# One-hot factors of an adjacency build split as quarter and place, and strip sums made by adding transfers

## The reference, cut to what matters

```python
summed = segment_sum(h[src], dst, num_segments=n)
count = segment_sum(ones(50000), dst, num_segments=n)[:, None]
out = (summed / maximum(count, 1.0)) @ W_agg.T + h @ W_lin.T
x = x + out / maximum(norm(out, axis=-1, keepdims=True), 1e-12)
```

## Time and profile before

| | |
|---|---|
| median of 3 runs | 3345.48 us (3345.35 to 3350.49) |
| span of the profiled execution, first to last instruction | 3347.6 us |
| build, first to last matmul (L538 on 128x400) | 360.40 to 848.27 us |
| granted TensorE clock, mean over the span | 0.824 |

### The profile page before, as it was taken

One profiled execution on the slowest core, in us unless ns is written; L12 is line 12 of the kernel. 1 busy time (PEld: TensorE's weight loads), 2 busy tenths in 40 slices (PEclk: granted clock), 3 DMA queues, 4 the chain that ended last, 5 costly groups with the idle time before them and its releaser, 6 DMA issues.

```text
span 3347.6 us, 46752 instructions
## 1 busy us (share of the span) xinstructions
PE 2186.4 (65%) x12603; PEld 1297.7 (39%) x12659; DVE 2262.1 (68%) x3125; ACT 846.9 (25%) x1397; POOL 1645.1 (49%) x1455
## 2 busy tenths in 40 slices
PE   0488877777895989995963444444567665528563
PEld 0233455454453455553443111111366621107563
DVE  8999898898558720055133454444987799979777
ACT  0099433232002020022100111111244322206442
POOL 7400133333047777777104777777876777710000
PEclk9799999999997999997986555565559999965897
DMA  2000010110443523400724433345348733530453
GB/s 71 0 0 0 25 49 39 44 44 39 148 137 84 164 60 96 94 1 1 158 59 94 117 113 112 112 116 104 93 153 268 240 110 110 107 37 0 134 175 94
DMA packets 195115, 301.52 MB, mean 90 GB/s; under 512 B 120540, under 2 KB 133818, under 8 KB 194922
## 3 DMA queue, kind: packets, MB, share of 16 engines
q1 hardware_dynamic: 138986, 175.88, 16.5%
q0 software_dynamic: 40512, 62.87, 10.3%
q10 hardware_dynamic: 15552, 61.94, 6.0%
HBM read 191.65 MB, written 88.01 MB: 84 GB/s over the span
## 4 chain that ended last, share of the span: by engine, by line
PE 35%; POOL 19%; issue 16%; DVE 16%; DMA 6%; ACT 5%; ACTq 1%; DVEq 0%; SPq 0%; POOLq 0%; PEldq 0%
POOL arena L1313 18%; PE PS L538 11%; PE PS L699 9%; PE PS L884 6%; DMA arena<-T_att,idx 5%; ACT arena L514 4%; DVE arena L559 4%; PE PS L981 3%; PE PS L476 2%; DVE arena L1204 1%; PE PS L968 1%; DVE arena L374 1%; DVE arena L490 1%; POOL W L1322 1%; DVE arena L567 1%
## 5 line engine op out<-in xcount | busy, mean ns | idle before, releaser
L1313 POOL DMA_INDIRECT arena<-T_att,idx x864 | 843.7, 976 | 316.9 <-issue 224.8
L538 PE MATMUL PS<-arena 128*128 128x400 f16 (+2 forms) x4320 | 782.5, 332 | 270.0 <-issue 109.7
L538 PEld LDWEIGHTS PS<-arena 128*128 128x128 f16 (+2 forms) x4320 | 529.9, 158 | 512.9 <-issue 349.8
L1148 DVE TENSOR_REDUCE arena<-PS 128x1024 f32 (+1 forms) x432 | 502.2, 1212 | 321.6 <-PE PS L1115 321.6
L1486 POOL DMA_INDIRECT order<-arena x400 | 504.8, 1262 | 246.5 <-issue 246.5
L559 DVE TENSOR_SCALAR arena<-arena 128x1600 f16<-128x1600 f16 x448 | 385.7, 905 | 64.4 <-PE PS L538 60.4
L1115 PE MATMUL PS<-arena,pick 128*128 128x512 bf16 x812 | 315.8, 488 | 157.0 <-DVE arena L1148 143.2
L699 PE MATMUL PS<-arena 128*128 128x512 f16 (+1 forms) x1575 | 317.6, 361 | 88.3 <-issue 75.2
L633 POOL TENSOR_TENSOR rdeg<-rdeg,arena 128x1600 f32<-128x1600 f32 x48 | 159.9, 3331 | 313.4 <-ACT arena L617 313.4
L1104 PE MATMUL PS<-ident_b,score_buf 128*32 128x128 bf16 x864 | 90.0, 268 | 307.1 <-ACT score_buf L1077 297.4
L699 PEld LDWEIGHTS PS<-arena 128*128 128x128 bf16 x1575 | 147.8, 99 | 254.1 <-issue 102.3
(11 more groups left out here) (257 smaller groups left out, 2786.0 us busy)
## 6 DMA issues: line engine op xcount, KB each, us to landing
spill<-arena SPq DMA_DIRECT2D x108, 560.0 KB, 2.8
arena<-spill ACTq DMA_DIRECT2D x108, 560.0 KB, 3.9
arena<-A SPq DMA_DIRECT2D x50, 800.0 KB, 4.5
A<-arena SPq DMA_DIRECT2D x50, 400.0 KB, 2.4
arena<-A SPq DMA_DIRECT2D x50, 400.0 KB, 3.2
arena<-T_att,idx POOLq DMA_INDIRECT x864
order<-arena POOLq DMA_INDIRECT x400
T_att<-h SPq DMA_DIRECT2D x2, 1600.0 KB, 12.3
```

The lines of the kernel that those rows point to most:

```text
L538: return t.matmul(where, lhsT, rhs, start=False, stop=True, skip_group_check=True)
L1148: v.tensor_reduce(cmax[d][:, u:u + 2, bass.ds(i * SLOTS + half * GROUP + q // 2 * QUAD, QUAD)], PS[:, u * BANK:(u + 2) * BANK].rearrange(" ...
L1313: p.indirect_dma_start(out=ring1[:, b, j, :], out_offset=None, in_=T_att[d][:, :], in_offset=bass.IndirectOffsetOnAxis(ap=idx[:, d, k:k + ...
```

## The change

For each edge the band's 1,600 places are split as quarter and place in the quarter: `hi_i` = 0 to 3, `dst_low` = `dst_in` - 400 * quarter. The quarter moves into the other factor: `src_quarter` = source place + 128 * quarter. The factors of a chunk are now a 512-wide one-hot of `src_quarter` and a 400-wide one-hot of `dst_low`, both by `tensor_scalar`, in rings of 8. The four matmuls of a chunk take four different weights (128 contiguous columns each) and the same 400 columns. The sources' own instruction for 8 chunks and its semaphore are gone. `dst_sum` is cleared by a memset on POOL, and each `stage` buffer is added to it by a DMA that POOL issues and that adds as it writes (`accum_op`, fp16 read, fp32 sum); an add waits for the add of two cells before, which has the same destination. ACT reuses a `stage` buffer when both its store and its add have landed; what waited for `cell_counted` waits for all adds.

```diff
-        RING_D, RING_S, RING_A = 4, 2, 4
+        RING_D, RING_A = GROUP, 4
+        QW = BW // BQ
...
             def chunk(i, s, first):
                 if not first:
                     v.wait_ge(chunk_done, RING_D * i + s - RING_D + 1)
-                v.tensor_scalar(oh_d[s], steps_h, dst_in[:, bass.ds(RING_D * i + s, 1)], None, ALU.is_equal) \
-                    .then_inc(dst_ready, 1)
-            def sources(i, s, first):
-                if not first:
-                    v.wait_ge(chunk_done, (RING_S * i + s - RING_S + 1) * GROUP)
-                c = bass.ds((RING_S * i + s) * GROUP, GROUP)
-                v.tensor_tensor(oh_s[s], iota_8, key_h[:, c].unsqueeze(1).to_broadcast([P, P, GROUP]), ALU.is_equal) \
-                    .then_inc(src_ready, 1)
+                c = bass.ds(RING_D * i + s, 1)
+                v.tensor_scalar(oh_s[s], steps_h[:, 0:BQ * P], src_quarter[:, c], None, ALU.is_equal)
+                v.tensor_scalar(oh_d[s], steps_h[:, 0:QW], dst_low[:, c], None, ALU.is_equal).then_inc(dst_ready, 1)
             v.wait_ge(sorted_ready, 1)
-            v.tensor_copy(iota_8, steps_h[:, 0:P].unsqueeze(2).to_broadcast([P, P, GROUP]))
-            dve_link(v.tensor_copy(key_h, key[:, 1, :]))
+            dve_link(v.tensor_scalar(hi_i, dst_in, float(QW), None, ALU.is_ge))
+            for q in range(2, BQ):
+                dve_link(v.scalar_tensor_tensor(hi_i, dst_in, float(q * QW), hi_i, ALU.is_ge, ALU.add))
+            v.scalar_tensor_tensor(src_quarter, hi_i, float(P), key[:, 1, :], ALU.mult, ALU.add)
+            dve_link(v.scalar_tensor_tensor(dst_low, hi_i, -float(QW), dst_in, ALU.mult, ALU.add))
...
-            with t.Fori(0, GR[1] // RING_S) as i:
-                for s in range(RING_S):
-                    g = RING_S * i + s
...
+            with t.Fori(0, CH[1] // RING_D) as g:
+                turn = load_row(t, cell_turn[:, bass.ds(g * RING_D, RING_D)], 1, BQ * BANK * (BANDS - 1) + CELLS)
+                for j in range(RING_D):
+                    t.wait_ge(slot_free, turn[j] & 63)
+                    t.wait_ge(dst_ready, g * RING_D + j + 1)
+                    for b in range(BQ):
+                        last = add_to(t, PS[:, bass.ds((turn[j] & (BQ * BANK)) + b * BANK, QW)],
+                                      oh_s[j][:, b * P:(b + 1) * P], oh_d[j])
+                    last.then_inc(chunk_done, 1)
...
                     a.wait_ge(a_written[c % RING_A], 16 * (c // RING_A))
-                    a.wait_ge(cell_counted, c - RING_A + 1)
+                    a.wait_ge(cell_added[c % RING_A], 16 * (c // RING_A))
...
             p.wait_ge(lo_ready, 1)
+            pool_link(p.memset(dst_sum, 0.0))
             for c in range(CELLS):
                 at = dst_sum[:, c % BANDS * BW:(c % BANDS + 1) * BW]
                 p.wait_ge(cell_out, c + 1)
-                if c < BANDS:
-                    p.tensor_copy(at, stage[c % RING_A]).then_inc(cell_counted, 1)
-                else:
-                    p.wait_ge(cell_counted, c - BANDS + 1)
-                    p.tensor_tensor(at, at, stage[c % RING_A], ALU.add).then_inc(cell_counted, 1)
+                if c >= BANDS:
+                    before = c - BANDS
+                    p.wait_ge(cell_added[before % RING_A], 16 * (before // RING_A + 1))
+                p.dma_start(out=at, in_=stage[c % RING_A], accum_op=ALU.add).then_inc(cell_added[c % RING_A], 16)
```

More of the change, by code:

```diff
@@ L199, in gnn_kernel @@
         dst_in = view(6656, CH[1])
-        RING_D, RING_S, RING_A = 4, 2, 4
-        oh_d = [view(7200 + s * BW // 2, BW // 2).bitcast(F16) for s in range(RING_D)]
-        oh_s = [view(10400 + s * GROUP * P // 2, GROUP * P // 2).bitcast(F16).rearrange("p (c j) -> p c j", j=GROUP)
-                for s in range(RING_S)]
+        RING_D, RING_A = GROUP, 4
+        QW = BW // BQ
+        src_quarter, dst_low, hi_i = view(0, CH[1]), view(CH[1], CH[1]), view(2 * CH[1], CH[1])
+        oh_d = [view(7200 + s * QW // 2, QW // 2).bitcast(F16) for s in range(RING_D)]
+        oh_s = [view(8800 + s * BQ * P // 2, BQ * P // 2).bitcast(F16) for s in range(RING_D)]
         stage = [view(11424 + s * BW // 2, BW // 2).bitcast(F16) for s in range(RING_A)]
-        iota_8 = view(14624, GROUP * P // 2).bitcast(F16).rearrange("p (c j) -> p c j", j=GROUP)
-        key_h = view(14624 + GROUP * P // 2, CHUNKS // 2).bitcast(F16)
         blk = view(20800, 8 * BLK).rearrange("p (x o c n) -> p x o c n", x=2, o=2, c=2)
@@ L282, in gnn_kernel @@
         apart_ready, apart_seen = sem("apart_ready"), sem("apart_seen")
-        src_ready, dst_ready, chunk_done = sem("src_ready"), sem("dst_ready"), sem("chunk_done")
+        dst_ready, chunk_done = sem("dst_ready"), sem("chunk_done")
         cell_out, slot_free = sem("cell_out"), sem("slot_free")
-        cell_counted, dst_summed, dst_read = sem("cell_counted"), sem("dst_summed"), sem("dst_read")
+        dst_summed, dst_read = sem("dst_summed"), sem("dst_read")
+        cell_added = [sem(f"cell_added{s}") for s in range(RING_A)]
         a_written = [sem(f"a_written{s}") for s in range(RING_A)]
@@ L558, in chunk @@
                     v.wait_ge(chunk_done, RING_D * i + s - RING_D + 1)
-                v.tensor_scalar(oh_d[s], steps_h, dst_in[:, bass.ds(RING_D * i + s, 1)], None, ALU.is_equal) \
-                    .then_inc(dst_ready, 1)
-            def sources(i, s, first):
-                if not first:
-                    v.wait_ge(chunk_done, (RING_S * i + s - RING_S + 1) * GROUP)
-                c = bass.ds((RING_S * i + s) * GROUP, GROUP)
-                v.tensor_tensor(oh_s[s], iota_8, key_h[:, c].unsqueeze(1).to_broadcast([P, P, GROUP]), ALU.is_equal) \
-                    .then_inc(src_ready, 1)
-            v.wait_ge(sorted_ready, 1)
-            v.tensor_copy(iota_8, steps_h[:, 0:P].unsqueeze(2).to_broadcast([P, P, GROUP]))
-            dve_link(v.tensor_copy(key_h, key[:, 1, :]))
-            per = GROUP // RING_D
-            for s in range(RING_S):
[L575 to L584, removed]
+                c = bass.ds(RING_D * i + s, 1)
+                v.tensor_scalar(oh_s[s], steps_h[:, 0:BQ * P], src_quarter[:, c], None, ALU.is_equal)
+                v.tensor_scalar(oh_d[s], steps_h[:, 0:QW], dst_low[:, c], None, ALU.is_equal).then_inc(dst_ready, 1)
+            v.wait_ge(sorted_ready, 1)
+            dve_link(v.tensor_scalar(hi_i, dst_in, float(QW), None, ALU.is_ge))
[3 more added lines that the diff above has]
+            dve_link(v.scalar_tensor_tensor(dst_low, hi_i, -float(QW), dst_in, ALU.mult, ALU.add))
+            for s in range(RING_D):
+                chunk(0, s, True)
+            with v.Fori(1, CH[1] // RING_D) as i:
+                for s in range(RING_D):
+                    chunk(i, s, False)
         def build_pe(t):
@@ L628, in count_pool, with all_added @@
                 p.wait_ge(cell_out, c + 1)
-                if c < BANDS:
-                    p.tensor_copy(at, stage[c % RING_A]).then_inc(cell_counted, 1)
-                else:
-                    p.wait_ge(cell_counted, c - BANDS + 1)
-                    p.tensor_tensor(at, at, stage[c % RING_A], ALU.add).then_inc(cell_counted, 1)
+                if c >= BANDS:
+                    before = c - BANDS
+                    p.wait_ge(cell_added[before % RING_A], 16 * (before // RING_A + 1))
+                p.dma_start(out=at, in_=stage[c % RING_A], accum_op=ALU.add).then_inc(cell_added[c % RING_A], 16)
+        def all_added(eng):
+            for s in range(RING_A):
+                eng.wait_ge(cell_added[s], 16 * len(range(s, CELLS, RING_A)))
         DEG_PIECES = HT_BLOCKS
@@ L642, in dst_degree_pe @@
             if m == 0:
-                t.wait_ge(cell_counted, CELLS)
+                all_added(t)
             else:
@@ L1523, in _ @@
             v.wait_ge(pads_written, 16)
-            v.wait_ge(cell_counted, CELLS)
+            all_added(v)
             place_dve(v, 0)
@@ L1741, in _ @@
             a.wait_ge(h_ready, 1)
-            a.wait_ge(cell_counted, CELLS)
+            all_added(a)
             ht_act(a, 0)
```

## The result

The changed kernel takes 3324.34 us (median of 4 runs, 3321.62 to 3325.36) against 3347.31 us (4 runs, 3345.35 to 3350.49): a ratio of 0.993 [0.9916, 0.9944], **0.7% faster**. The forecast was 3293 us, 52.5 us less; 23 us came. The sign is right. The time lies above the forecast's own range (3272 to 3312) and inside the wide one (3268 to 3345) only because that one takes in the second rival. The profiled execution, which the trace shows, went from a span of 3347.6 to 3323.5 us, 24.1 us less.

A forecast was written before the change was run, and what follows sets the result against it. PE's own instruction stream sets a floor of 423 us in the 487.9 us build, DVE's stalls in POOL's adds add most of the rest; -52.5 - 6 + 2.5 + 1 + 2.5 = -52.5 us gave 3293 us, range 3272 to 3312, wide 3268 to 3345.

The forecast's parts named there:

- the second rival: Build: adds take 8.6 to 10 us, PE waits behind ACT, which waits for buffers; around 3320 us, chance 0.08.
- The adds as transfers: Strip adds in the build, moved to DMA: 6.4 us each, hidden behind PE, so 0 us of cost.
- rivals 1 to 3: Build: adds from 10.0 us bound it, 3405 us (0.14); the second rival (0.08); POOL can't issue, 4.6 ms (0.02).
- The strip adds leave POOL: Build: DVE is no longer stopped by POOL and PE runs at its own pace, 435.4 against 487.9 us: -52.5 us.
- the comparisons: DVE in the build: 0.51 us a chunk against 0.65, faster than PE's 0.8 anyway, so no gain by itself.
- PE's pace, -52.5 us: Build: 55 group steps of 7.80 us and a last 6.44 us make 435.4 us, against 487.9.
- The weights, -6 us: PE's weight loads in the build, now contiguous: 98 in place of 146 ns; -6 us, bounds -21 and 0.
- rival 4: Build: contiguous weights let PE's chunks go at their columns' pace, 54 us gained in place of 6; 3245 us, chance 0.04.
- The memset, +2.5 us: Sort stage: POOL's memset of 128 x 3200 stops DVE's comparisons; +2.5 us, bounds 0 and 2.9.
- The five instructions ahead of the build, +1.0 us: Before the build: five 448-column instructions, some 3.0 us, where 1.7 us were; +1.0 us, bounds 0 and 2.
- The end, +2.5 us: Behind the build: last store and first strip loads share DMA engines with the last adds; +2.5 us, bounds 0 and 5.

## Why the prediction was wrong in size

**The step that failed** is "The adds as transfers ... So **0 us** as long as an add takes less than about 8.6 us of the DMA engines." I asked only who waits for an add to end (ACT for a buffer, PE, DVE and ACT behind the last one), and there the answer was right: an add lands in 5.3 us (taken: 6.4), its issue takes 0.86 us (taken: 1), ACT waited for none of them (all 313.6 us of its wait are for PE, in the row of L599 above), and rivals 1 to 3 did not come. I did not ask who reads SBUF while an add runs. PE does, once a group, on its own path: +20.4 us of the build (454.4 against 434.1 with POOL's adds). The prediction had named that load as 0.9 to 1.3 us of PE's pace and taken it as fixed.

That 3324 us lies near the 3320 of the second rival, and so inside the wide range, is luck: the condition of that rival was adds of 8.6 us and more, with ACT waiting for buffers.

One reading beside this step is wrong too. By the earlier trace rows POOL's queue does not have the shorter rows: 62.87 MB in 40,512 packets are 1.55 KB each, 175.88 MB in 138,986 are 1.27 KB. The 6.4 us rest on that reading. By the share of POOL's queue with adds (15.3% of 3323.5 us) and without (10.6% of 3293.7 us), an add took about 3.2 us of the DMA engines, half of the 6.4.

**A second step was wrong without changing the sum**: "The strip adds leave POOL. That is what pays", and of the comparisons "this edit pays nothing by itself". The runs show that the two halves of the change remove the same wait, DVE's stops in POOL's adds; the first hides them under a ring of 8, the second takes them away:

| build, us | adds by POOL | adds by transfer |
|---|---|---|
| old factors, ring of 4 | 487.9 | 446.3 |
| new factors, ring of 8 | 434.1 | 454.4 |

The new factors with their ring of 8 give all of the 53.8 us by themselves. On top of them the transfers have nothing left to remove and cost 20.4 us. On top of the transfers the new factors cost 8.1 us, since they put a branch at every group; with PE's loop over two groups they save 4.9 us there (441.4). Most of the 53.8 us is the ring: with the new factors and a ring of 4 the build takes 473.9 us, so 39.9 us come with the depth and 14.0 us without it. The old factors with a ring of 8 were not run.

The other terms, by their own measure:

- **PE's pace, -52.5 us**: right. 434.1 or 434.2 us of build where no transfer adds, against 435.4.
- **The weights, -6 us**: near 0. Loads fell from 146 to 99 ns, but 32 matmuls at the full clock take 6.38 to 6.44 us, where they took 6.44 to 6.50; 56 times 0.06 us would be 3 us at most, and they are part of the pace above. The chunks did not come down to their columns' pace, so rival 4 fell as well. The Trainium skill ("TensorE: Matmul & The Clock Gate", section "Weight-path perf modes") counts a step of 8 elements between columns as fit for the fast load, by which this term is 0. The time agrees with that; the durations of 146 and 99 ns do not, but here the loads are hidden.
- **The memset, +2.5 us**: 2.6 (DVE's L503 came 3.9 us later than L504 before, 1.3 of them from the sort, where an instruction ahead of all that changed, 130.84 us before, began at 132.10; in the other runs it begins at 130.7 to 132.1).
- **The five instructions ahead of the build, +1.0 us**: 1.3, from there to the first matmul.
- **The end, +2.5 us**: 2.6, the strip load of 11.16 us.

Together: -53.8 + 20.4 + 2.6 + 1.3 + 2.6 = -26.9 us; with 1.3 us of the sort and 1.7 us behind the build, both of the size by which runs of one kernel differ, -23.9 of the 24.1 us of span.

**Open** stays why an adding transfer holds up a load of 32 bytes from SBUF. Shown is that a copy of the same bytes to another address hardly does it, even where load and transfer stand at the same times, that it needs no add on the load's own partition, though the half that holds this partition costs more, and that it goes when the add runs at another time. Whether it is the adding itself or its destination is not shown: an add whose destination lies elsewhere, or two copies in its place, were not tried.

## What to carry to other kernels

Work that is moved to DMA is not free when it is hidden: besides who waits for it, ask which small reads of the same memory lie on the bounding engine's path while it runs, here the register loads of PE's sequencer, which the busy times of a page do not show. Two edits that remove the same wait do not add up; price each alone against that wait, and what each brings, before they go in together. A deeper ring was here the better half: it hid stops of 3.2 us that the transfers were meant to take away, and the version that stopped there (3296 us, and 3278 us with longer rows of turns) beats both kernels.

## What the hardware showed that was not expected

- PE's load of 8 registers from SBUF takes 0.59 us, of 16 1.11 us. Beside an adding transfer one of 8 took up to 1.81 us (with the old factors; 2.59 us beside adds of 64 partitions); beside copies 1.20 us at most. With no transfer on POOL's queue it took 1.13 us at most with the new factors, and 1.23 us in the kernel before.
- An adding transfer from SBUF to SBUF, 128 x 1600 fp16 onto fp32, lands in 5.3 us, with 64 partitions in 5.4 us; the same as a copy in 4.2 us. Its issue on POOL takes 0.86 us, a copy's 0.53 us, among two comparisons of 0.32 to 0.35 us on DVE for each chunk.
- A branch of PE's loop costs 0.34 to 0.38 us here.
- A group of 8 chunks took 7.74 us from start to start with a stretch at the lower clock level in it (its matmuls lasted 7.42 us) and 7.74 us at the upper level throughout (6.42 us).
